# Loads issued inside the layer norms, and three layers of a twelve-layer decoder rearranged

## The chip, the cores and the metric

One Trainium2 chip, one of its cores. The metric is the device time of the whole kernel in microseconds; the median of three runs is 5381.53 us.

## What is computed

A pre-norm decoder of four levels with three layers each, on x of 32 sequences x 64 tokens x 256 features (2048 tokens), in float32:

```python
x = x + L0_attn(norm(x)); x = x + L0_xattn(norm(x), ctx); x = x + L0_ffn(norm(x))
x = x + L1_attn(norm(x)); x = x + L1_xattn(norm(x), ctx); x = x + L1_ffn(norm(x))
x = x + L2_attn(norm(x)); x = x + L2_xattn(norm(x), mask, ctx); x = x + L2_ffn(norm(x))
x = x + L3_attn(norm(x)); x = x + L3_xattn(norm(x), ctx); x = x + L3_ffn(norm(x))
# L0_xattn, a recurrence per channel (k = norm(x), v = ctx), along 64 tokens
no = max(o, u + k); A = exp(o - no); E = exp(u + k - no); y = (A*p + E*v) / (A*q + E)
no2 = max(w + o, k); A2 = exp(w + o - no2); E2 = exp(k - no2)
p, q, o = A2*p + E2*v, A2*q + E2, no2
# L2_ffn: weights are 4-bit codes with one scale per 32 (values 0 .5 1 1.5 2 3 4 6 and a sign)
gelu = tanh(0.79788 * (gate + 0.044715 * gate**3)) * gate * 0.5 + gate * 0.5
out = (gelu * up) @ Wd.T                       # hidden width 2048
# L3_xattn
s = sigmoid(decay) * s + (ctx @ W_in.T + b_in)  # scan over 64 tokens
y = norm(x) + mean(s @ W_out.T + b_out); out = layernorm(y) * gamma + beta
```

## The kernel before

X, XN, XT and CT (the stream, its norm, the norm turned with channels on partitions, and the context turned) stay in SBUF for the whole program. Tokens lie in 16 tiles of 128 or 4 chunks of 512; channels in two halves of 128.
In the layer's Block SyncE issues the loads, and the other engines wait for the sum of them: `attention` (L235, used three times: l0_attn, l1_attn, l2_xattn), `l1_xattn`, `l2_attn`, `l3_attn`, `l3_xattn`, `l3_ffn`. `l3_ffn`, a mixture of experts, issues its small gate weights and then 26 transfers of 384 KB.

`l0_xattn` (L737) runs the recurrence on one channel half after the other, on all 2048 tokens per instruction: a running maximum by one scan, the shifted maximum by a copy (L776), differences, four exponentials on ScalarE, two scans for the sums, denominator, `reciprocal` (L800) on VectorE, numerator, quotient, TensorE transposes (L831), adds into X (L808).

`l2_ffn` (L1702) first turns all codes of gate, up and down weights into float32 on VectorE, nine operations of 2048 elements per nibble and matrix, reloading one pair of buffers between the matrices. Then it loops over 4 chunks and 16 hidden tiles. A unit is: gate and up product (L1815), Square on ScalarE, a scalar and a tensor product on VectorE, Tanh on ScalarE, two more products on VectorE (L1777, L1781), and the down product with the tokens as fixed operand (L1826), one unit late.

`l3_xattn` (L2406) projects the context for 2048 tokens, copies it out, scans it and sums it per sequence, for each channel half; then a loop over 16 tiles broadcasts the means, multiplies by W_out (L2455), adds the bias by a matmul of one row (L2456), adds XN, and normalizes with gain and offset, one tile after the other.

## Time and profile before

| | |
|---|---|
| median of three runs | 5381.53 us (5368.63 to 5385.0) |
| profiled execution, its own time | 5369.39 us |
| its span | 5367.6 us |
| TensorE matmul busy | 4292.7 us, 80% |
| VectorE busy | 3443.4 us, 64% |
| ScalarE busy | 2078.4 us, 39% |
| GpSimd busy | 1218.2 us, 23% |
| mean granted TensorE clock | 0.901 of full speed |

Where the layers begin, by the first statistics of their norm, in us: 36.3, 245.7, 390.9, 505.7, 742.6, 928.3, 1025.6, 1651.8, 2037.0, 2508.5, 4587.6, 4767.9. The shares are averages over layers that have different limits, so a layer is read by its own stretch of the timeline.

### The profile page before, as it was taken

What the parts mean: (1) busy time and instruction counts of PE and PEld (TensorE: products, weight loads), DVE (VectorE), ACT (ScalarE), POOL (GpSimd) and SP (SyncE); (2) the same over time, 40 slices, a digit from 0 to 9 for tenths busy, and PEclk for the clock granted to TensorE, in tenths of its full rate; (3) what the DMA queues carried; (4) which work ended last, traced back from release to release, by engine and by line L of the source; (5) the groups of instructions that cost most, each with busy time, mean ns of one, the idle gap of its engine ahead of it and who ended that gap; (6) DMA issues with size and microseconds to landing.
All of it is one profiled execution on the core that took longest, in us unless ns stands there. A gap on an engine that the chain in (4) does not pass through costs nothing. (4 is left out here: it accounts for less than half of the span.)

```text
span 5367.6 us, 147544 instructions
## 1 busy us (share of the span) xinstructions
PE 4292.7 (80%) x62322; PEld 2855.3 (53%) x62330; DVE 3443.4 (64%) x6320; ACT 2078.4 (39%) x3687; POOL 1218.2 (23%) x1233
## 2 busy tenths in 40 slices
PE   5705777577766881898999999999999999459998
PEld 4603645323324661455576766667676767235554
DVE  4797643678886776544787877778787877331111
ACT  3415442544443551122454544445454444111110
POOL 0100200088893220000222222222222221002222
PEclk9957888788898995998999999999999999559999
DMA  1000000023331001000000000000000000021111
GB/s 45 1 0 33 1 11 0 35 107 121 123 133 37 1 1 47 0 0 18 9 11 11 11 11 13 11 11 11 11 11 11 17 5 3 6 93 52 49 49 47
DMA packets 60767, 157.48 MB, mean 29 GB/s; under 512 B 11890, under 2 KB 19060, under 8 KB 58868
## 3 DMA queue, kind: packets, MB, share of 16 engines
q1 hardware_dynamic: 60180, 148.91, 8.2%
q8 instruction: 459, 7.52, 0.6%
q14 instruction: 128, 1.05, 0.1%
HBM read 146.26 MB, written 2.62 MB: 28 GB/s over the span
## 5 line engine op out<-in xcount | busy, mean ns | idle before, releaser
L2262 POOL TENSOR_TENSOR dn_eb<-dn_ee,dn_cc 128x512 f32<-128x512 f32 x64 | 66.8, 1043 | 1470.0 <-DVE dn_cc L2368 1470.0
L2722 DVE TENSOR_TENSOR moe_hh<-moe_si,moe_pu 128x512 f32<-128x512 f32 x104 | 71.4, 687 | 451.7 <-PE moe_pu L2611 445.4
L1634 POOL TENSOR_TENSOR ssm_ub<-ssm_dtu,ssm_bcn 128x512 f32<-128x512 f32 x256 | 319.5, 1273 | 26.3 <-DVE ssm_ph L1693 24.5
L1986 PE MATMUL dn_bA<-core_XT,dn_w 128*128 128x512 f32 x512 | 268.7, 650 | 45.8 <-issue 40.8
L2298 DVE SCALAR_TENSOR_TENSOR core_XN<-dn_bA,dn_w,core_XN 128x504 f32<-128x504 f32 (+2 forms) x384 | 280.6, 731 | 28.4 <-ACT core_XN L2155 8.8
L2674 POOL TENSOR_TENSOR moe_hw<-moe_hh,moe_cb 128x512 f32<-128x512 f32 x100 | 126.9, 1269 | 681.1 <-DVE moe_hh L2722 393.6
L1595 ACT ACTIVATE ssm_da<-core_XN,ssm_al 128x504 f32<-128x504 f32 x256 | 173.9, 683 | 262.0 <-DVE ssm_ph L1693 142.5
L2655 ACT ACTIVATE moe_si<-moe_pg 128x512 f32<-128x512 f32 x104 | 62.2, 598 | 468.2 <-PE moe_pg L2611 468.2
L2117 PE MATMUL dn_po<-dn_wo,dn_cT 128*128 128x256 f32 x1024 | 239.8, 387 | 1.7 <-ACT dn_cT L2215 1.1
L1532 PE MATMUL ssm_py<-ssm_hc,core_ident 128*128 128x512 f32 x320 | 193.5, 709 | 55.3 <-DVE ssm_hc L1697 30.4
L1693 DVE TENSOR_TENSOR_SCAN ssm_ph<-ssm_da,ssm_ub 128x512 f32<-128x512 f32 x160 | 195.1, 1219 | 53.4 <-ACT ssm_da L1595 22.3
L1815 PE MATMUL nv_pg<-core_XT,nv_wg 128*128 x256 | 122.2, 600 | 116.9 <-PEq L1804 116.9
L2010 PEld LDWEIGHTS dn_pm<-dn_zz,dn_XB 32*32 32x32 f32 x16384 | 165.0, 105 | 93.0 <-issue 91.7
L2245 POOL TENSOR_TENSOR dn_gm<-dn_gg,dn_msk 128x256 f32<-128x256 f32 x128 | 87.5, 703 | 536.6 <-DVEq L2291 534.9
L2010 PEld LDWEIGHTS dn_pm<-dn_XB,dn_mb 32*32 32x32 f32 x16384 | 164.7, 105 | 81.5 <-issue 73.0
L2117 PEld LDWEIGHTS dn_po<-dn_wo,dn_cT 128*128 128x128 f32 x1024 | 190.9, 191 | 28.2 <-ACT dn_cT L2215 1.5
L2268 POOL TENSOR_TENSOR dn_mb<-dn_BD,dn_small 128x256 f32<-128x256 f32 x256 | 190.2, 773 | 50.4 <-DVE dn_BD L2380 50.4
L2611 PE MATMUL moe_pg<-core_XT,moe_w 128*128 128x512 f32 x416 | 198.6, 600 | 0.0
L2010 PE MATMUL dn_pm<-dn_XB,dn_mb 32*32 32x32 f32 x16384 | 193.2, 194 | 6.3 <-DVE dn_XB L2309 3.1
L2611 PE MATMUL moe_pu<-core_XT,moe_w 128*128 128x512 f32 x416 | 196.2, 594 | 0.0
L2010 PE MATMUL dn_pm<-dn_zz,dn_XB 32*32 32x32 f32 x16384 | 193.7, 194 | 1.2 <-ACT dn_zz L2164 1.0
L1532 PE MATMUL ssm_py<-ssm_hp,core_ident 128*128 128x512 f32 x192 | 118.0, 699 | 93.3 <-POOL ssm_hp L1625 93.1
(500 smaller groups left out, 10594.5 us busy)
## 6 DMA issues: line engine op xcount, KB each, us to landing
ssm_bcn<-ssm_bct SPq DMA_DIRECT2D x128, 512.0 KB, 3.6
dn_w<-in_dn_w SPq DMA_DIRECT2D x16, 776.0 KB, 5.3
moe_cb<-moe_rows SPq DMA_DIRECT2D x64, 192.0 KB, 2.8
moe_w<-in_moe_w SPq DMA_DIRECT2D x26, 384.0 KB, 10.5
moe_cb<-moe_rows SPq DMA_DIRECT2D x64, 128.0 KB, 3.0
dn_wo<-in_dn_w SPq DMA_DIRECT2D x16, 256.0 KB, 2.7
moe_cb<-moe_rows SPq DMA_DIRECT2D x64, 64.0 KB, 2.6
core_X<-in_x SPq DMA_DIRECT2D x1, 2048.0 KB, 8.7
```

Source lines behind the costliest of these rows:

```text
L1532: pe.matmul(py[:, turn_ % 2, :], g.ident[:, :], src[:, :], start=n == 0, stop=n == N - 1).then_inc(add_done, 1)
L1595: act.activation(nb(da[:, u % 2, :])[:, :, 1:S], nb(dt[q % 2][:, c, :])[:, :, 1:S], ACT.Exp, scale=al[:, n, c:c + 1]).then_inc(da_ready, 1)
L1634: pool.tensor_tensor(ub[u % NUB][:, :], dtu[q % 2][:, c, :], bcn[i % NB][:, 0, :], ALU.mult).then_inc(ub_ready, 1)
L1693: dve.tensor_tensor_scan(ph[:, m % 2, :], da[:, u % 2, :], ub[u % NUB][:, :], 0.0, ALU.mult, ALU.add).then_inc(scan_done, 1)
L1815: mm = pe.matmul(dst[:, q, :], w[:, kc, cs], g.XT[:, kc, bass.ds(i * CH, CH)], start=kc == 0, stop=kc == DC - 1)
L1986: mm = pe.matmul(bank[:, :], wp[:, kc, gi * P:(gi + 1) * P], g.XT[:, kc, q * CH:(q + 1) * CH], start=kc == 0, stop=kc == DC - 1)
L2010: mm = pe.matmul(bank[r, n * HB:(n + 1) * HB], left(n, r), right(n, r), start=True, stop=True, tile_position=(q * HB, q * HB))
L2117: mm = pe.matmul(po[:, j // 2, (j % 2) * D:(j % 2 + 1) * D], cT[:, 2 * j + h, :], wo[o // NCH % 2][:, h, :], start=h == 0, stop=h == 1)
L2268: pool.tensor_tensor(halves(mb[i % 2][:, l - 1, :]), BD[:, :, :], bcm(small[:, 1 + l, :], NS), ALU.mult).then_inc(mb_ready, 1)
L2298: last = dve.scalar_tensor_tensor(dst[:, :, n:S], src[:, :, 0:S - n], w[i // NCH % 2][:, at:at + 1], dst[:, :, n:S], ALU.mult, ALU.add)
L2611: mm = pe.matmul(dst[:, m % 2, :], w[:, k, at:at + P], g.XT[:, kc, n * CH:(n + 1) * CH], start=kc == 0, stop=kc == DC - 1)
L2674: pool.tensor_tensor(hw[m % 3][:, :], hh[m % 3][:, :], cb[j % NCB][:, :], ALU.mult).then_inc(hw_ready, 1)
```

## The change

- `layer_norm` takes a function `early`, which SyncE runs in the norm's Block. All layers issue their loads by it. Buffers and the semaphores of the loads are made ahead of the norm, in a group of their own; the rest behind it.
- `l0_xattn`: both channel halves in each phase: maxima of both, sums of both, quotients, adds. The shifting copy goes to ScalarE; the reciprocal becomes Ln and Exp(-x) on ScalarE. The load of w and u is issued in the norm.
- `l2_ffn`: the weights are cut into 8 blocks of 256 code columns (all three matrices, both nibbles at once). Blocks 0 and 1 are loaded in the norm. VectorE has six wide operations and four shifts per block, ScalarE two. Tokens go in two halves of two chunks; in the first half the next block is unpacked in four pieces, one in each unit, between the unit's `inner` and `outer`. The down product now has the weights as the fixed operand and 512 tokens as the moving one, two units late; its sums are turned back by transposes (`T` items) at the end of each half.
- `l3_xattn`: four chunks; projection, scan, sum, broadcast, output, statistics and normalization of different chunks overlap; statistics are taken for four tiles at a time; the normalization goes to ScalarE, gain and offset to GpSimd.
- The other layers differ only in where the loads are issued.

```diff
-def layer_norm(nc, g, tag, step=1, turned=True):
+def layer_norm(nc, g, tag, step=1, turned=True, early=None):
...
+            @block.sync
+            def _(sp):
+                if early is not None:
+                    early(sp)
...
+        def early(sp):
+            for dst, name in consts:
+                sp.dma_start(dst[tuple(slice(None) for _ in dst.shape)], w[name]).then_inc(w_loaded, 16)
...
+        layer_norm(nc, g, norm, early=early)
...
+        def early(sp):
+            sp.dma_start(wu[:, :, :], a["wkv_wu"]).then_inc(loaded, 16)
+        layer_norm(nc, g, "0x", early=early)
...
+        om, op, no, a2, e2 = [[s.sb(f"{n}{c}", [P, TOK]) for c in range(DC)] for n in ("om", "op", "no", "a2", "e2")]
+        e1 = [xn[:, c, :] for c in range(DC)]
...
+                def maxima(c):
+                    k = g.XT[:, c, :]
...
                     dve.drain()
+                    dve.tensor_tensor_scan(om[c][:, :], ws[:, :], k, NEG_INIT, ALU.add, ALU.max).then_inc(max_ready, 1)
                     dve.drain()
+                    dve.tensor_tensor(e2[c][:, :], k, om[c][:, :], ALU.subtract)
+                    dve.wait_ge(prev_ready, c + 1)
+                    dve.scalar_tensor_tensor(no[c][:, :], k, u, op[c][:, :], ALU.add, ALU.max)
+                    dve.scalar_tensor_tensor(a2[c][:, :], op[c][:, :], w, om[c][:, :], ALU.add, ALU.subtract).then_inc(decay_ready, 1)
                     dve.drain()
+                    dve.scalar_tensor_tensor(e1[c], k, u, no[c][:, :], ALU.add, ALU.subtract).then_inc(own_ready, 1)
+                    dve.tensor_tensor(no[c][:, :], op[c][:, :], no[c][:, :], ALU.subtract).then_inc(prior_ready, 1)
...
+                def sums(c):
+                    v = g.CT[:, c, :]
+                    dve.wait_ge(exp_ready, c + 1)
...
+                    dve.tensor_tensor(om[c][:, :], no[c][:, :], qb[:, 0:TOK], ALU.mult)
+                    dve.tensor_tensor(om[c][:, :], om[c][:, :], e1[c], ALU.add).then_inc(den_ready, 1)
+                    dve.tensor_tensor(op[c][:, :], no[c][:, :], pb[:, 0:TOK], ALU.mult)
+                    dve.tensor_tensor(tv[:, :], e1[c], v, ALU.mult)
+                    dve.tensor_tensor(op[c][:, :], op[c][:, :], tv[:, :], ALU.add)
+                def quotient(c):
...
+                maxima(0)
+                maxima(1)
+                sums(0)
+                sums(1)
+                quotient(0)
+                quotient(1)
+                added(0)
+                added(1)
...
+                def previous(c):
+                    act.wait_ge(max_ready, c + 1)
+                    act.activation(by_batch(op[c])[:, :, 1:S], by_batch(om[c])[:, :, 0:S - 1], ACT.Copy).then_inc(prev_ready, 1)
...
+                def reciprocals(c):
+                    act.wait_ge(den_ready, c + 1)
+                    act.activation(om[c][:, :], om[c][:, :], ACT.Ln)
+                    act.drain()
+                    act.activation(om[c][:, :], om[c][:, :], ACT.Exp, scale=-1.0).then_inc(rcp_ready, 1)
+                previous(0)
+                exponentials(0)
+                previous(1)
+                exponentials(1)
+                reciprocals(0)
+                reciprocals(1)
...
+    H, BW, NW, NIT = 2048, 256, 3, 3
+    NBLK = H // BW
+    W1 = 2 * NW * BW
...
+        def codes_in(sp, b):
+            for k, n in enumerate("gud"):
+                sp.dma_start(pk[b % 2][:, k, :], a[f"nv_{n}_packed"][:, b * BW:(b + 1) * BW]).then_inc(pk_loaded[b % 2], 16)
+                sp.dma_start(scl[b % 2][:, k, :], a[f"nv_{n}_scales"][:, b * BW:(b + 1) * BW]).then_inc(pk_loaded[b % 2], 16)
+        def early(sp):
+            codes_in(sp, 0)
+            codes_in(sp, 1)
+        layer_norm(nc, g, "2f", step=2, early=early)
...
+                for b in range(2, NBLK):
+                    sp.wait_ge(scaled, b - 1)
+                    codes_in(sp, b)
...
+                for k in range(len(items) + 2):
+                    if k >= 2:
+                        pe.wait_ge(done, k - 1)
+                    if k < len(items) and items[k][0] == "U":
...
+                        gate_up(k, b, (2 * h + i) * CH, n)
+                    if k >= 2 and items[k - 2][0] == "U":
+                        down(k - 2)
+                    if k < len(items) and items[k][0] == "T":
+                        turn(k)
...
+                def parts(b):
...
+                    act.wait_ge(code_ready, b + 1)
+                    if b:
+                        act.wait_ge(w_ready, b)
+                    act.activation(t1[:, :], flat3(mi[:, :, :, :]), ACT.Identity, bias=cst[:, 0:1], scale=2.0).then_inc(part_ready, 1)
+                    act.activation(flat3(sgn[:, :, :, :]), flat3(si[:, :, :, :]), ACT.Identity, bias=cst[:, 1:2], scale=-2.0).then_inc(sign_ready, 1)
+                parts(0)
...
+                def codes(b):
+                    dve.wait_ge(pk_loaded[b % 2], 2 * NW * 16 * (b // 2 + 1))
+                    if b:
+                        dve.wait_ge(w_ready, b)
+                    src = pk[b % 2][:, :, :]
+                    for nib in range(2):
+                        dve.tensor_scalar(mi[:, nib, :, :], src, 4 * nib, 7, ALU.arith_shift_right, ALU.bitwise_and)
+                        dve.tensor_scalar(si[:, nib, :, :], src, 4 * nib + 3, 1, ALU.arith_shift_right, ALU.bitwise_and)
+                    dve.drain().then_inc(code_ready, 1)
+                def sizes(b):
+                    dve.wait_ge(part_ready, b + 1)
+                    dve.scalar_tensor_tensor(t1[:, :], flat3(mi[:, :, :, :]), -2.0, t1[:, :], ALU.add, ALU.max)
+                    dve.drain()
+                    dve.scalar_tensor_tensor(t1[:, :], flat3(mi[:, :, :, :]), 0.5, t1[:, :], ALU.mult, ALU.max)
+                def scales(b):
+                    dve.wait_ge(sign_ready, b + 1)
...
+                    dve.tensor_tensor(both, both, bcm(scl[b % 2][:, :, :].rearrange("p b c -> p (b c)"), 2), ALU.mult).then_inc(scaled, 1)
+                def weights(b):
+                    dve.drain()
+                    dve.tensor_tensor(flat3(w[:, b, :, :, :]), t1[:, :], flat3(sgn[:, :, :, :]), ALU.mult).then_inc(w_ready, 1)
...
+                        inner(k)
+                        if h == 0 and b + 1 < NBLK:
+                            if (i, n) == (0, 0):
+                                codes(b + 1)
+                            if (i, n) == (0, 1):
+                                sizes(b + 1)
+                            if (i, n) == (1, 0):
+                                scales(b + 1)
+                            if (i, n) == (1, 1):
+                                weights(b + 1)
+                        outer(k)
...
+        loads = [(dec, "lk_decay"), (wi, "lk_wi"), (bi, "lk_bi"), (wo, "lk_wo"), (bo, "lk_bo"), (gb, "lk_gb")]
+        nl = 16 * len(loads)
+        def early(sp):
+            for dst, n in loads:
+                sp.dma_start(dst[tuple(slice(None) for _ in dst.shape)], a[n]).then_inc(loaded, 16)
+        layer_norm(nc, g, "3x", turned=False, early=early)
...
+                for n in range(NCH):
+                    for oc in range(DC):
+                        chunk(n, oc)
+                    if n >= 1:
+                        output(n - 1)
+                output(NCH - 1)
...
+                def based_on(i):
+                    pool.tensor_tensor(group(g.X, i), group(g.X, i), bcm(gb[:, 1, :], TPC), ALU.add).then_inc(based, 1)
+                def gain(i):
+                    pool.wait_ge(norm_ready, i + 1)
+                    pool.tensor_tensor(group(g.XN, i), group(g.XN, i), bcm(gb[:, 0, :], TPC), ALU.mult).then_inc(gained, 1)
+                for i in range(NCH):
+                    based_on(i)
+                for i in range(NCH):
+                    gain(i)
...
+                def states(n):
+                    for oc in range(DC):
+                        k = n * DC + oc
+                        dve.wait_ge(xi_ready, k + 1)
+                        dve.tensor_tensor_scan(st[k % 2][:, :], kd[:, :], xi[k % 3][:, :], 0.0, ALU.mult, ALU.add).then_inc(scan_done, 1)
                         dve.drain()
+                        dve.tensor_reduce(ms[:, oc, n * BC:(n + 1) * BC], by_batch(st[k % 2][:, :]), AX.X, ALU.add)
                     dve.drain()
+                    if n >= 2:
+                        dve.wait_ge(y_ready, n - 1)
+                    for oc in range(DC):
+                        last = dve.tensor_scalar(by_batch(mr[n % 2][:, oc, :]), bc(ms[:, oc, n * BC:(n + 1) * BC], S), 1.0 / S, None, ALU.mult)
                     last.then_inc(mr_ready, 1)
+                def stats(i):
+                    dve.wait_ge(y_ready, i + 1)
+                    dve.tensor_tensor(group(g.XN, i), group(g.XN, i), py[:, i % 2, :, :], ALU.add).then_inc(y_done, 1)
                     dve.drain()
+                    for t in range(i * TPC, (i + 1) * TPC):
+                        dve.bn_stats(bs[:, t, :], g.XN[:, t, :])
                     dve.drain()
+                    for t in range(i * TPC, (i + 1) * TPC):
+                        last = dve.bn_aggr(mv[:, t, :], bs[:, t, :])
+                    last.then_inc(stats_ready, 1)
...
+                def added(i):
+                    dve.wait_ge(based, i + 1)
+                    dve.wait_ge(gained, i + 1)
+                    dve.tensor_tensor(group(g.X, i), group(g.X, i), group(g.XN, i), ALU.add)
+                states(0)
+                states(1)
+                stats(0)
+                states(2)
+                means(0)
+                stats(1)
+                states(3)
+                means(1)
+                stats(2)
+                added(0)
+                means(2)
+                stats(3)
+                added(1)
+                means(3)
+                added(2)
+                added(3)
...
+        def early(sp):
+            sp.dma_start(gw[:, :, :], a["moe_gate"]).then_inc(c_loaded, 16)
+            for k in range(G):
+                sp.dma_start(w[:, k, :], a["moe_w"][k, :, :]).then_inc(w_loaded[k], 16)
+        layer_norm(nc, g, "3f", early=early)
```

## Rows read from the trace of the kernel before

**Rows 1.** Timeline, first TensorE instruction of six layers; start, length, idle before.

```profile
58.59 1.87 PE L460 MATMUL a_pm<-a_wo,a_bcol 128*1 128x256 f32 x4 [9.16 <-PEq L296]
...
526.60 3.50 PE L366 MATMUL a_pm<-core_XT,a_wqk 128*128 128x128 f32 x16 [6.95 <-PEq L296]
...
764.55 5.71 PE L1163 MATMUL lin_pr<-core_XT,lin_wq 128*128 128x512 f32 x8 [8.82 <-DMA lin_wo<-in_lin_wo]
...
1049.46 6.61 PE L1501 MATMUL ssm_pp<-core_XT,ssm_win 128*128 128x512 f32 x8 [10.77 <-DMA ssm_vec<-in_ssm_vec]
...
1675.74 3.75 PE L366 MATMUL a_pm<-core_XT,a_wqk 128*128 128x128 f32 x16 [10.82 <-PEq L296]
...
2527.40 13.91 PE L1965 MATMUL dn_po<-dn_wab,core_XT 128*128 128x64 f32 x64 [5.80 <-DMA dn_lt<-in_dn_later]
```

**Rows 2.** Timeline of the recurrence, second channel half.

```profile
327.15 1.76 DVE L768 MEMSET wkv_ws<- 128x2048 f32 x1 [0.38 <-issue]
...
335.07 1.21 DVE L776 COPY wkv_op<-wkv_om 128x2016 f32<-128x2016 f32 x1
...
343.31 1.91 ACT L815 ACTIVATE wkv_a<-wkv_a 128x2048 f32<-128x2048 f32 x1 [54.85 <-ACTq L814]
...
367.89 12.95 DVE L800 RECIPROCAL wkv_om<-wkv_om 128x2048 f32<-128x2048 f32 x1
...
385.50 3.65 PE L831 MATMUL wkv_pt<-core_ident,wkv_yT 128*128 128x128 f32 x16 [59.56 <-PEq L827]
...
389.30 0.69 DVE L808 TENSOR_TENSOR core_X<-core_X,wkv_pt 128x512 f32<-128x512 f32 x1 [0.17 <-DVEq L806]
```

**Rows 3.** The four-bit layer: groups by line, then timeline.

```profile
L1769 DVE TENSOR_SCALAR nv_sq<-nv_sq 128x512 f32<-128x512 f32 x64 | 27.3, 426 | 91.7 <-DVEq L1768 91.5
L1752 DVE SCALAR_TENSOR_TENSOR nv_t<-nv_t 128x2048 f32<-128x2048 f32 x6 | 13.8, 2292 | 0.5
...
2051.89 1.28 ACT L1790 ACT_TABLE_LOAD   x1 [1.47 <-PEq L74]
...
2167.13 3.78 PE L1815 MATMUL nv_pg<-core_XT,nv_wg 128*128 x4 [116.86 <-PEq L1804]
...
2183.14 1.88 PE L1815 MATMUL nv_pg<-core_XT,nv_wg 128*128 x4
...
2188.30 1.88 PE L1815 MATMUL nv_pg<-core_XT,nv_wg 128*128 x4
...
2505.99 1.22 DVE L1786 TENSOR_TENSOR core_X<-core_X,nv_py 128x1024 f32 x1 [2.46 <-DVEq L1783]
```

**Rows 4.** Timeline of the last cross attention: start, cold matmuls, first and last add.

```profile
4599.90 0.34 SPq L2437 DMA_DIRECT2D lk_wi<-in_lk_wi  x1
...
4605.02 8.90 PE L2448 MATMUL lk_pp<-core_CT,lk_wi 128*128 128x512 f32 x16 [22.12 <-DMA lk_dec<-in_lk_decay]
...
4640.47 2.04 PE L2455 MATMUL lk_py<-lk_wo,lk_mr 128*128 128x256 f32 x4 [10.16 <-PEq L2453]
...
4647.49 0.42 DVE L2526 TENSOR_TENSOR core_X<-core_X,lk_z 128x256 f32 x1
...
4766.40 0.42 DVE L2526 TENSOR_TENSOR core_X<-core_X,lk_z 128x256 f32 x1
```

**Rows 5.** Timeline of the last layer's start: SyncE's issues, the first matmuls.

```profile
4782.63 0.33 SPq L2580 DMA_DIRECT2D moe_gw<-in_moe_gate  x1
4783.01 19.01 SPq L2582 DMA_DIRECT2D moe_w<-in_moe_w  x26
...
4784.44 13.86 PE L2598 MATMUL moe_py<-moe_gw,core_XT 128*128 128x32 f32 x64 [3.43 <-DMA moe_gw<-in_moe_gate]
```

**Rows 6.** Tile core_X, last norm: ns minimum, median, maximum; first and last start.

```profile
L154 DVE BATCH_NORM_STATS2 ln3f_st<-core_X x16: 395/410/427, 4767.9 to 4774.9; 128x6 f32<-128x256 f32 x16
```

**Rows 7.** Timeline of l3_attn, VectorE and GpSimd started together.

```profile
3004.88 1.59 POOL L2268 TENSOR_TENSOR dn_mb<-dn_BD,dn_small 128x256 f32<-128x256 f32 x2 [0.79 <-DVE dn_BD L2380]
3004.89 0.99 DVE L2383 TENSOR_TENSOR dn_b<-dn_BD,dn_small 128x256 f32<-128x256 f32 x1
```

567 lines of the change are left out of this document (267 added, 300 removed).

## The prediction

> **What bounds the kernel now.** I read the busy row of the page first, then the listing of one tile (core_X, which every layer reads at its start and writes at its end) to cut the span into layers, then the timeline at each boundary, and for the rebuilt layers the groups by line. TensorE is the busiest engine, but the change touches mostly stretches where it waits: twelve layers stand one behind the other with a barrier of all engines between them, so the time is a sum over layers, and each piece is to be read where it runs. Four kinds of stretch matter. First, behind a normalization the next layer issues its loads and all engines wait for them [rows 1]. Second, the recurrence is a single VectorE chain, twice, with a 12.95 us reciprocal in each [rows 2]. Third, in the four-bit layer TensorE stands idle 116.86 us while VectorE unpacks weights [rows 3]; then it is the bound, one unit of work every 5.16 us. Fourth, in the last cross attention one 128-token tile goes through PE, VectorE, ScalarE and VectorE before the next may start, 16 times [rows 4].
>
> **Early loads, six layers where a wait goes.** PE's idle time before its first instruction was 9.16, 6.95, 8.82, 10.77, 10.82 and 5.80 us [rows 1], 52.3 together. Not all is the load: in the last layer the first issue is at 4782.63, PE starts at 4784.44 and had been idle 3.43, so the barrier takes 1.62 of it [rows 5]. Less 6 x 1.62, 42.6 us go. SyncE issued 26 large transfers in 19.0 us, 0.73 each, so the ten at most of these layers take 7.3, and a normalization lasts 14 (4767.9 [rows 6] to 4782.6): the data are there. I take -42. Bounds: 0 if something else (code, a table) was as late as the data; -47 if TensorE also keeps the high clock it has at the end of a normalization. The two ternary feed-forward layers gain nothing, since VectorE first reduces other data there.
>
> **The loads of the last layer.** Here the early issue costs. SyncE needed 19.0 us to issue 26 weight transfers, from 4783.01 [rows 5]: the issues block. It now does this inside the normalization, whose end is a barrier that includes SyncE. From 4767.9 [rows 6] that is 4767.9 + 0.4 + 19.0 = 4787.3; with the hand-over of 0.9 PE starts at 4788.2, where it started at 4784.44: +3.8 us (bounds: -1.8, the wait for moe_gw alone, if the issues went faster; +6).
>
> **Semaphores.** A scope clears each group of semaphores that it made in a block of its own. Ten layers now make one group more, and 25 or so semaphores are added. Behind the last cross attention a hand-over with one such block takes 4766.82 to 4767.9, 1.1 us [rows 4, 6], so one block costs between 0 and 1.1; I take a third, +3.5 us (bounds 0 and 11).
>
> **The recurrence.** Old: from the second half's start at 327.15 to the last add, 389.30 + 0.69, is 62.8 us, twice 125.7 plus 0.4 between them, 126.1 [rows 2]. Removed from VectorE: two reciprocals (25.9) and two shifting copies at 1.2 (2.4). ScalarE's stand-in for a reciprocal, Ln and Exp, costs 2 x 1.91 and begins when the denominator is ready, with three VectorE operations (6.8 us) and the quotient of the other half still to come: hidden. ScalarE's copy (1.9, as its Exp) runs under the subtraction of 2.3 us: hidden, by 0.2. The transposes and adds behind each half, from 385.50 to 389.99, now overlap for one half: -3.5. The wait for the small load goes, as in the six layers: -1.6, since one transfer lands sooner than ten. Sum -33 (bounds -30, if the hand-overs through ScalarE show, and -35).
>
> **The four-bit layer.** Old: from 2051.89 to 2505.99 + 1.22, 455.3 us [rows 3]. New: the same 64 units of 5.16 us, 330; none of the matmul work changes but the down product, which takes 512 columns with a fixed weight, the same columns. Ahead of it only block 0 is unpacked. A block has 1536 elements per partition and operation. At 2.29 us per 2048 a two-input operation takes 1.72: four of them, 6.9; the four shifts of 768 cost at most 0.43 x 1.5 = 0.6 each, 2.1 together; waiting for ScalarE's part (1536 x 1.91 / 2048 = 1.4) and drains, 2.2. So PE starts 11.2 us into the layer, and its cold start costs 2. Then one block of codes is unpacked per four units. VectorE's own share per unit is 0.43 + 3 x 0.69 = 2.5 (0.69 from the add in [rows 2]), with drains 2.8; four units and a block make 20.0 us, PE's four units 20.6. That is nearly equal, so the order decides. I laid the instructions out one after another: `codes` of the next block lies before the unit's `outer`, ScalarE's two parts (2.9 us) follow and delay the next unit's Square by 2, VectorE idles for that long, then `sizes` (3.5) delays that unit, and the last, `weights`, ends 3 us after PE wanted it. Period 23.5 instead of 20.6, seven times: +20. The half's end (two turns of the sums, each ScalarE's copy 1.0, sixteen transposes 1.9 at the high clock, where they took 3.65 cold [rows 2], and adds 1.4) costs 8.6, the layer's end 7.6. Sum 11.2 + 2 + 330 + 20 + 8.6 + 7.6 = 379: -76. Bounds: if VectorE hid fully, -96; if the 9.0 us of pieces lay fully bare in each block, 7 x (9.0 - 2.9) = 43 more, -33.
>
> **The last cross attention.** Old: from 4599.90 to 4766.40 + 0.42, 166.9 us, of which the 16 rounds are 4766.40 - 4647.49 = 118.9 for fifteen [rows 4]. New, again laid out in order: eight chunks of 4 matmuls. Sixteen took 8.90 us starting cold, five of them at the low clock, so 0.43 each warm: a chunk 1.7. An output step has 24 matmuls of 256 columns: 0.49 each cold (2.04 for four, with a tail), a quarter of 1 us warm, 6 us. PE: 8 x 1.7 + 4 x 6 + 2 = 40. VectorE per group: two scans at 4.42 / 4 = 1.2, two reductions and two broadcasts of 0.7, sum 5.2; statistics 1.2 + 4 x 0.41 + 0.4 = 3.2 (0.41 from [rows 6], the last an estimate); added 1.2: 38 in all. They alternate and end at 43; behind the last output stand the last group's statistics, its Ln and Exp, four ScalarE normalizations (2.1), GpSimd's product (2.4) and an add: 10. So 53. GpSimd now works beside VectorE. A VectorE product of 128x256 that began with two GpSimd instructions took 0.99 us [rows 7], where such a product takes 0.42 [rows 4]; it was held up. Eight GpSimd instructions of some 2.4 us (an estimate: 0.8 for 256 elements in that row, here 1024, less their fixed part) can each hold up one VectorE operation; most fall where VectorE waits anyway, I add 2. Total 55: -112, of which 5 is the load. The Trainium skill, page "SBUF — State Buffer", section "SBUF: two separate sides", speaks against the change here: a GpSimd instruction and a VectorE one that reads two SBUF tensors exclude each other for a whole instruction. By that rule the scans, which read kd and xi from SBUF, wait for up to eight whole GpSimd instructions, and the layer would end at 72 instead of 55; by the row's 0.57 us of delay each it would be 58. Bounds: -117, and, PE at the low clock throughout, 87 us: -80.
>
> **Sum.** -42 + 3.8 + 3.5 - 33 - 76 - 112 = -256, with 2 us for clocks kept high -258, from 5369.4 for the profiled execution (span 5367.6): 5111. The median of the three runs lies 12 us higher, at 5381.5, within a spread of 16; from there it is 5124. I say 5122.
>
> **Rivals.**
> A. TensorE stays at 1.2 GHz in the last cross attention. For it: its output steps are cold today [rows 4]; against: they come after waits, the first of 10.16 us, and would wait 1 us at most. Layer 87 instead of 55: 5154.
> B. VectorE's pieces in the four-bit layer are bare: each block waits through Square, `inner`, a piece, `outer`. For it: the sum is within 3% of PE's. +43: 5165.
> C. The moved loads don't do what they are to: at each layer's start something else is as late. For it: nothing shows what engines would have done without the data; against: the last normalization's first instruction comes 1.1 us behind the add of the layer before, barriers included. +42: 5164.
> D. GpSimd's eight instructions each hold VectorE up for their whole 2.4 us: 19 us instead of the 2 in the sum, +17, 5139. For it: the product that took 0.99 [rows 7]; against: it lost 0.57, not the 0.8 of its neighbour, and VectorE waits for TensorE anyway in part of the layer. This is the case of the Trainium skill's page "SBUF — State Buffer".
> E. Slower than before: the stalls on block hand-overs leave TensorE at the low clock in the four-bit layer. A unit of three groups then takes 10.3 us, and all 64 cost +330: 5122 + 330 = 5452. It decides from 50 units on (258 / 5.16). Against: only 8 of 64 units would have a wait of over 1 us before them.
>
> **How the numbers follow.** Forecast 0.66, A 0.09, B 0.09, C 0.06, D 0.08, E 0.01, no effect or other 0.01. The forecast's own range is 5122 -24 +22: -20 if the blocks hide, -5 clocks; the runs' spread of 16; +11 semaphores and hand-overs. It holds D. For the whole, 5095 to 5158 takes in A and leaves B, C and E out, some 17 in 100. 0.3% of the time is 16 us, which a measurement here can tell from nothing. Faster 0.98, same 0.01, slower 0.01.
>
> **What would show it.** In the profile after: the idle time of PE ahead of the first matmul behind a normalization near 1.6 us in six layers; the last normalization's end at some 19.5 us behind its start; the four-bit layer near 380, its first matmul 11 us in, the block period in its first half 23.5 and the clock at 1.0 there; the last cross attention near 55 with output steps of 6 us; recurrence near 93. Wrong would be made most easily by the order of VectorE's queue in the two pipelined layers, which I laid out by hand with hand-overs of 0.1 to 0.25 us.

## The result, and the profile after

The changed kernel takes 5104.53 us (median of four runs, 5095.46 to 5111.69), the kernel before 5379.23 in the same session: ratio 0.949, 95% interval 0.948 to 0.950, 275 us less. The profiled execution has a span of 5105.5 us against 5367.6 (-262.1) and a mean granted clock of 0.925 in place of 0.901. Forecast were 5122 and 5095 to 5158: the time lies 17 below the first and inside the second.

The span was cut into layers as before, by the first statistics of each norm in the listing of tile core_X (layer and norm together, us; "same kernel again" is after profiled a second time):

| layer | before | after | same kernel again | difference before to after | forecast |
|---|---|---|---|---|---|
| l0_attn | 209.4 | 199.4 | 199.6 | -10.0 | -7.5 |
| l0_xattn (recurrence) | 145.2 | 110.7 | 110.7 | -34.5 | -33 |
| l0_ffn | 114.8 | 115.4 | 115.5 | +0.6 | 0 |
| l1_attn | 236.9 | 229.8 | 226.8 | -7.1 | -5.3 |
| l1_xattn | 185.7 | 182.2 | 177.9 | -3.5 | -7.2 |
| l1_ffn | 97.3 | 96.9 | 96.9 | -0.4 | 0 |
| l2_attn | 626.2 | 616.1 | 616.2 | -10.1 | -9.1 |
| l2_xattn | 385.2 | 377.8 | 377.7 | -7.4 | -9.2 |
| l2_ffn (four-bit) | 471.5 | 385.0 | 384.9 | -86.5 | -76 |
| l3_attn (delta net) | 2079.1 | 2084.9 | 2090.4 | +5.8 | -4.2 |
| l3_xattn | 180.3 | 70.1 | 78.2 | -110.2 | -112 |
| l3_ffn | 599.7 | 601.1 | 600.9 | +1.4 | +3.8 |

The forecast column gives each wait of [rows 1] less 1.62; 3.5 for clearing semaphores and -2 for clocks come to the sum besides.

**Early loads.** Timeline after, the first TensorE instruction of the six layers; the number in brackets is TensorE's idle time before it, which was 5.80 to 10.82 in [rows 1]:

```profile
51.05 1.87 PE L467 MATMUL a_pm<-a_wo,a_bcol 128*1 128x256 f32 x4 [1.80 <-PEq L310]
...
476.55 2.02 PE L373 MATMUL a_pm<-core_XT,a_wqk 128*128 128x128 f32 x16 [1.81 <-PEq L310]
...
706.24 5.37 PE L1198 MATMUL lin_pr<-core_XT,lin_wq 128*128 128x512 f32 x8 [1.66 <-PEq L74]
...
985.41 3.67 PE L1540 MATMUL ssm_pp<-core_XT,ssm_win 128*128 128x512 f32 x8 [1.66 <-PEq L74]
...
1602.41 2.02 PE L373 MATMUL a_pm<-core_XT,a_wqk 128*128 128x128 f32 x16 [1.81 <-PEq L310]
...
2365.42 13.89 PE L2081 MATMUL dn_po<-dn_wab,core_XT 128*128 128x64 f32 x64 [1.66 <-PEq L74]
```

What is left is the barrier. Counted from each norm's start, TensorE begins 7.3, 5.9, 7.1, 8.9, 8.1 and 2.9 us sooner, 40.2 together.

**The last layer** pays, as forecast: SyncE's issues, now in the norm, and the wait in front of the first matmul that they cause (timeline after; [rows 5] has the same before):

```profile
4504.69 17.49 SPq L2729 DMA_DIRECT2D moe_w<-in_moe_w  x26
...
4523.25 13.83 PE L2786 MATMUL moe_py<-moe_gw,core_XT 128*128 128x32 f32 x64 [5.76 <-PEq L74]
```

The norm starts at 4504.4, so TensorE begins 18.9 us behind it; before it was 4784.44 - 4767.9 = 16.5.

**The recurrence.** From 250.78, the instruction at which the 126.1 us of the prediction begin, to the end of the last add at 344.67 it takes 93.9 us (93 forecast). ScalarE's stand-in for the reciprocal waits for VectorE and never the other way round; the adds now are one run of eight:

```profile
250.78 1.76 DVE L774 MEMSET wkv_ws<- 128x2048 f32 x1 [0.40 <-issue]
...
306.07 1.91 ACT L848 ACTIVATE wkv_om<-wkv_om 128x2048 f32<-128x2048 f32 x1 [13.08 <-DVE wkv_om L801]
...
339.81 4.86 DVE L816 TENSOR_TENSOR core_X<-core_X,wkv_pt 128x512 f32<-128x512 f32 x8
```

**The four-bit layer.** Timeline after: the layer's begin, its first matmul, and the waits for the product of the next block ([rows 3] has the layer before):

```profile
1979.66 1.28 ACT L1840 ACT_TABLE_LOAD   x1 [1.46 <-PEq L74]
...
1990.82 3.78 PE L1802 MATMUL nv_pg<-core_XT,nv_w 128*128 128x512 f32 x4 [12.78 <-DVE nv_w L1896]
...
2015.22 1.96 PE L1802 MATMUL nv_pg<-core_XT,nv_w 128*128 128x512 f32 x4 [1.74 <-DVE nv_w L1896]
...
2037.80 1.96 PE L1802 MATMUL nv_pg<-core_XT,nv_w 128*128 128x512 f32 x4 [1.74 <-DVE nv_w L1896]
...
2060.39 1.96 PE L1802 MATMUL nv_pg<-core_XT,nv_w 128*128 128x512 f32 x4 [1.74 <-DVE nv_w L1896]
```

TensorE starts 11.2 us in, as laid out. A later block then takes 22.59 us, 2.0 more than four units, and it always ends with the same wait; the first block, with TensorE cold at its start, takes 24.40.

**The last cross attention.** Timeline after: GpSimd's four additions beside the first scans, two of which are long, and the first output step.

```profile
4446.66 11.29 POOL L2636 TENSOR_TENSOR core_X<-core_X,lk_gb 128x1024 f32<-128x1024 f32 x4 [67.62 <-SPq L2559]
...
4451.19 1.40 DVE L2664 TENSOR_TENSOR_SCAN lk_st<-lk_kd,lk_xi 128x512 f32<-128x512 f32 x1 [1.72 <-ACT lk_xi L2603]
...
4453.28 2.54 DVE L2664 TENSOR_TENSOR_SCAN lk_st<-lk_kd,lk_xi 128x512 f32<-128x512 f32 x1
...
4458.50 1.21 DVE L2664 TENSOR_TENSOR_SCAN lk_st<-lk_kd,lk_xi 128x512 f32<-128x512 f32 x1
```

And windows of that layer (length, busy time with number of instructions of PE, PEld, DVE, ACT, POOL, then the granted clock): the projections start cold, the first output step is at 1.00.

```profile
4446.60:4458.50 11.90, 9.12 (x16) 3.75 (x16) 8.56 (x12) 4.24 (x6) 11.29 (x4) 0.83 0.00 0
4458.50:4469.00 10.50, 10.37 (x33) 5.60 (x34) 7.48 (x16) 0.30 (x1) 0.00 (x0) 1.00 0.01 2
```

### The profile page after: what moved, and what is told of

The parts are those of the page before. It is cut to its first block and busy times, and to the rows that moved or that the text cites. A ratio compares the mean times of both kernels' runs of the same rounds, so it can differ in the third digit from the quotient of the medians.

```text
span 5105.5 us, 146480 instructions
## 1 busy us (share of the span) xinstructions
PE 4270.6 (84%) x62098; PEld 2796.8 (55%) x62106; DVE 3363.6 (66%) x6251; ACT 2120.9 (42%) x3712; POOL 1236.9 (24%) x1241
## 5 line engine op out<-in xcount | busy, mean ns | idle before, releaser
L2414 DVE SCALAR_TENSOR_TENSOR core_XN<-dn_bA,dn_w,core_XN 128x504 f32<-128x504 f32 (+2 forms) x384 | 280.5, 731 | 30.6 <-ACT core_XN L2271 8.8
L2280 ACT ACTIVATE dn_zz<-dn_pm 128x256 f32<-128x256 f32 x320 | 122.6, 383 | 170.0 <-PE dn_pm L2126 158.8
```

The source lines that it names most:

```text
L2414: last = dve.scalar_tensor_tensor(dst[:, :, n:S], src[:, :, 0:S - n], w[i // NCH % 2][:, at:at + 1], dst[:, :, n:S], ALU.mult, ALU.add)
```

## The experiments

Layer times are read as in the table above. Ratios are to the kernel before. All but loads_only, one_clear and best are one execution each, so only their layers are read, not their whole time.

**loads_only.** The kernel after, with the old `l0_xattn`, `l2_ffn` and `l3_xattn`.

> The kernel after, but with the recurrence, the four-bit layer and the last cross attention as they were before, their loads in their own Blocks; the nine other layers issue their loads inside the norm. My theory: each layer is a sum of its own, so this kernel gains what those nine layers gained between the two profiles, 30.7 us (the layers from 0a to 3f without the three: -10.0, +0.6, -7.1, -3.5, -0.4, -10.1, -7.4, +5.8, +1.4), a span near 5337 and a ratio of 0.994. My prediction had -42 for six waits and +3.8 for the last layer, with some +3 for clearing semaphores: -35, 5332. Rival: the delta-net layer's +5.8 hangs on what lies ahead of it (the four-bit layer's end, the clock there); then that layer is back at some 2075 here and the span near 5328. Rival 2: early loads bring nothing by themselves, 5369.

5337.73 us, ratio 0.992 (0.991 to 0.994), span 5334.7, 32.9 less than before. The nine other layers together gained 32.1 (-30.7 between before and after), so the layers together are a sum. Single layers agree less well: l0_attn gained 7.1 here and 10.0 in after, l1_xattn 6.7 and 3.5. The delta-net layer took 2082.5, again longer than before; it does not hang on the four-bit layer ahead of it.

**moe_late.** Only the gate weights are loaded in the last norm:

```diff
         def early(sp):
             sp.dma_start(gw[:, :, :], a["moe_gate"]).then_inc(c_loaded, 16)
-            for k in range(G):
-                sp.dma_start(w[:, k, :], a["moe_w"][k, :, :]).then_inc(w_loaded[k], 16)
...
             def _(sp):
+                for k in range(G):
+                    sp.dma_start(w[:, k, :], a["moe_w"][k, :, :]).then_inc(w_loaded[k], 16)
```

> The kernel after, but the 26 transfers of 384 KB of the last layer are issued in the layer's own Block again; only the gate weights are loaded in the norm. In the profile after, TensorE starts 18.85 us behind the norm's first statistics, with 5.76 us idle before it; before the change it was 16.54. My theory: SyncE's issues hold up the end of the norm's Block; with one issue there the first matmul comes 14.9 us behind the start of the norm, as in the other layers, and the layer takes 597 us in place of 601.1. Rival: the transfers now arrive later than the first groups of weights are wanted, and the gain is given back: layer 600 or more.

The layer took 596.8 us, 4.3 less. Timeline of moe_late:

```profile
4519.61 16.86 SPq L2770 DMA_DIRECT2D moe_w<-in_moe_w  x26
4519.65 13.54 PE L2786 MATMUL moe_py<-moe_gw,core_XT 128*128 128x32 f32 x64 [1.66 <-PEq L74]
```

The 26 issues run beside the gate's matmuls, TensorE starts 14.8 us behind the norm's first statistics in place of 18.9, and none of that is given back later in the layer. So the issue time of a queue counts where its engine must reach a barrier, and here it counted nowhere else.

**one_clear.** A scope clears all its semaphores in one Block, 55 Blocks fewer:

```diff
     def sem(self, *names):
...
-        self.ctx.callback(self.zero, s)
+        self.made += s
+        self.ctx.callback(self.zero)
-    def zero(self, sems):
+    def zero(self):
+        if self.cleared:
+            return
+        self.cleared, sems = True, self.made
```

> The kernel after, but a scope clears all semaphores that it made in one Block when it ends, in place of a Block for each group. 55 Blocks fall away, 33 of them behind the last layer, where from the end of the last add (5084.56) to the issue of the final store (5097.22) 12.66 us pass with 34 such Blocks. My theory: such a Block costs 12.66 / 34 = 0.37 us at most, about what I took (0.35), so -19 to -20 us in all, of which 11 to 12 between the last add and the store; span near 5086, ratio 0.9455. Rival: most of the 12.66 us is the end of the layer's Block and the clearing instructions themselves, which stay; then -5 us or less, span 5100.

5094.14 us, ratio 0.947 (0.946 to 0.949), against 0.949 for after: the intervals overlap, so the profile has to be read. Last adds and final store, first in after, then in one_clear:

```profile
5083.15 1.41 DVE L2901 TENSOR_TENSOR core_X<-core_X,moe_py 128x256 f32<-128x256 f32 x4 [4.44 <-PE moe_py L2814]
5097.22 0.41 SPq L2943 DMA_DIRECT2D out<-core_X  x1
```

```profile
5073.22 1.41 DVE L2906 TENSOR_TENSOR core_X<-core_X,moe_py 128x256 f32<-128x256 f32 x4 [4.43 <-PE moe_py L2819]
5078.11 0.41 SPq L2948 DMA_DIRECT2D out<-core_X  x1
```

12.66 us became 3.48: 9.2 us for 33 Blocks, 0.28 each. Less than the 11 to 12 that I expected, since 3.5 us of the stretch are not these Blocks. The span is 19.1 us below that of after, as I expected, but by luck: the delta-net layer took 10.9 less and the last cross attention 8.6 more, neither of them the Blocks' own time (below). In shifted (below) 20 such Blocks lengthened a hand-over from 2.26 us in best to 8.89, 0.33 each.

**weights_first.** In the four-bit layer the last piece goes ahead of the unit's `inner`:

```diff
+                        if h == 0 and b + 1 < NBLK and (i, n) == (1, 1):
+                            weights(b + 1)
                         inner(k)
```

> The kernel after, but in the four-bit layer the last piece of the next block (weights) lies ahead of the unit's inner in place of behind it. In the profile TensorE waits 1.74 us for that product at each of the blocks 1 to 7, and the period of a block is 22.59 us where four units take 20.6. My theory: the order of VectorE's queue makes the wait; moved ahead of inner (0.43 + 0.69 us and the wait for Square) the product is ready 1.4 us sooner, the wait falls to some 0.4, the period to 21.2 and the layer by 10 us: four-bit layer 375 in place of 385. Rival: VectorE's load is the cause, and the delay only moves into the unit's done, which TensorE waits for two units later: period 22.6 as before. Rival 2: it is better than that, since VectorE also waits for Tanh behind inner: 20.6, -14 us.

The layer took 380.3, 4.7 less; the wait fell from 1.74 to 0.65, but TensorE lost another 0.27 a unit earlier, period 21.87. Half of what I expected. In its timeline VectorE stood idle 2.04 us in each block for a Square that lay behind ScalarE's two parts, and this is what two_orders removes.

**no_beta, beta_twice, beta_late.** GpSimd's additions of the offset in the last cross attention left out, doubled, or placed behind the gains.

> The kernel after, but in the last cross attention GpSimd's four additions of the offset to X are left out (the offset is missing from the output). In the profile after, the first scans take 1.40 and 2.54 us in place of 1.2, two copies of means 1.90 in place of 0.76, and the four GpSimd instructions 2.8 each in place of the 2.35 of the later ones. My theory: the two engines slow each other down in part, some 2 to 3 us of VectorE's time in all, most of it ahead of the first output step; the scans fall to 1.22, the first output starts 2.5 us sooner (it was 11.98 us behind TensorE's first matmul) and the layer from 56 to 53.5. By the rule that a whole GpSimd instruction locks VectorE out, the lost time per scan would have been 2.35, and 4 to 9 us would come back. Rival: TensorE's chunks and not the scans set the start of the first output; then nothing changes.

Layer 67.9, first output at 22.24 us behind the norm's start in place of 24.33; the scans took 1.22 and 1.23. It gave 2.2 of the 2.5 us that I expected for the four additions.

> The kernel after, but GpSimd adds the offset to X twice in the last cross attention (the output has it twice), so four more GpSimd instructions of 2.4 us run beside the second and third groups of scans and the statistics. My theory: each costs VectorE 0.5 us or so, hidden in part by waits for TensorE: +0 to +2 us on the layer. If each locks VectorE out for its whole length, the layer is 5 to 9 us longer. Rival: gain of the first group waits behind the second pass in GpSimd's queue (it ends some 23 us behind the start of the layer, and the first gain was wanted about then), so that only the adds at the end shift, by less than 2 us.

80.2 us, more than any of the expectations, and most of it from a cause that I had not in view: the first output began 2.1 us later and ran at the low clock (1.55, then 2.08 us for four matmuls, in place of 1.13). So this run does not price the additions.

> The kernel after, but GpSimd adds the offset to X of a group behind the gain of that group, and only for the last group ahead of it; nothing of GpSimd lies beside the first scans. My theory: the first output starts 2.5 us sooner, as without the offset, and the four additions lie where VectorE waits for TensorE; the layer ends 1.5 to 2.5 us sooner. Rival: gain, addition, gain of 2.4 us each become late for the adds at the end, and the layer is as long as before or longer by up to 2.4 us.

73.7: longer by 3.6, a miss. The first output did start 2.5 us sooner, but GpSimd met VectorE later. Timeline of beta_late:

```profile
4483.21 2.36 POOL L2636 TENSOR_TENSOR core_X<-core_X,lk_gb 128x1024 f32<-128x1024 f32 x1
...
4483.98 2.67 DVE L2665 TENSOR_TENSOR_SCAN lk_st<-lk_kd,lk_xi 128x512 f32<-128x512 f32 x1 [1.22 <-ACT lk_xi L2603]
...
4492.44 2.35 POOL L2640 TENSOR_TENSOR core_XN<-core_XN,lk_gb 128x1024 f32<-128x1024 f32 x1 [6.87 <-ACT core_XN L2615]
...
4493.25 2.62 DVE L2694 TENSOR_TENSOR core_X<-core_X,core_XN 128x1024 f32<-128x1024 f32 x1
...
4494.75 3.32 POOL L2636 TENSOR_TENSOR core_X<-core_X,lk_gb 128x1024 f32<-128x1024 f32 x1
...
4495.79 2.30 DVE L2689 SCALAR_TENSOR_TENSOR lk_nm<-lk_mv,lk_rs 128x4 f32<-128x4 f32 x1
```

Each waits for the other's end. The scan ends at 4486.65, 1.08 us behind GpSimd's 4485.57, and takes 1.22 alone; the add ends 1.08 behind GpSimd's 4494.79; GpSimd's next takes 3.32 in place of 2.35; and an instruction on 128x4, 0.15 us elsewhere, takes 2.30 behind it. VectorE's add from PSUM (1.22, in after at 4492.56 us) and its statistics (1.41, beside GpSimd in both kernels) lost nothing. The Trainium skill, page "SBUF — State Buffer", section "SBUF: two separate sides", says that whichever of the two starts first holds the pair of ports for its whole instruction; the rows agree.

**dn_late.** The delta-net layer's loads in its own Block again (the old `l3_attn`).

> The kernel after, but the delta-net layer (3a) issues its loads in its own Block, as before. It was the one layer that took 5.8 us longer in the profile after, though TensorE started 2.9 us sooner: the norm took 1.3 more, the stretch from the first matmul to the first add 111.5 in place of 108.9, the 63 periods behind it 1952.1 in place of 1946.6. My theory: nothing of this comes from the moved loads but TensorE's clock after the four-bit layer's end and the loop's branches; then this kernel shows the norm still at 15 us, the loop still within 1946 to 1953, and the layer 2.9 us longer than in after, near 2088. Rival: the shorter wait shifts TensorE's clock in the prologue and the loop for the worse; then the layer is back at 2079 to 2081 here.

2093.5 us, 5.5 more than expected, with the first matmul 20.1 us behind the norm's start (16.0 in after). So the early load gains there too, and the rest, 1957.3 us for the 63 periods, is as long as in kernels that have the early load (1952.1 to 1960.8 in the eight others with as much code ahead of the layer); what lengthens the layer is elsewhere.

**after_again.** The same kernel once more.

> The kernel after once more, nothing changed: what its layers take in a second profile. So far the last cross attention took 70.1 us in after and in moe_late, 78.1 to 80.2 in weights_first, one_clear, dn_late and beta_twice, where TensorE's first output step (16 groups of matmuls, then the next two chunks) runs at the low clock (2.08 us for four matmuls in place of 1.13); in each of the six kernels TensorE had waited 2.0 to 4.8 us for the means ahead of it, and where the wait was 0.22 the clock stayed. The delta-net layer took 2074.0 to 2093.5 in kernels with the same code for it. My theory: whether the clock falls in that wait differs from one execution to the next; then the last cross attention is at 70 or 78 here, and the delta-net layer anywhere from 2080 to 2094. Rival: the same program gives the same clock in each layer; then both repeat within 1 us (70.1 and 2084.9), and the difference comes with each kernel's code.

Last cross attention 78.2, delta net 2090.4, l1_xattn 177.9 in place of 182.2. Timeline of after_again, the first output step and the chunks behind it:

```profile
4456.95 1.61 PE L2580 MATMUL lk_py<-lk_wo,lk_mr 128*128 128x256 f32 x4 [2.04 <-DVE lk_mr L2671]
...
4459.65 2.08 PE L2580 MATMUL lk_py<-lk_wo,lk_mr 128*128 128x256 f32 x4
...
4469.11 6.38 PE L2570 MATMUL lk_pp<-core_CT,lk_wi 128*128 128x512 f32 x8
```

The same instructions take 1.13 and 3.70 us in after. Of the seven profiles with a wait of about 2 us or more ahead of the first output, two kept the clock at 2.4 GHz (waits 2.83 and 2.59, layer 70.1 both) and five fell to 1.2 (waits 1.94 to 2.20, and 4.79 in beta_twice; layer 78.1 to 80.2). Three more kernels, below, fell in a wait of 2.5 to 3.1 us ahead of the fourth step. The length of the wait does not decide it. What TensorE did before it goes with it: in six of the seven profiles the projections begin 12.37 us behind the norm's start and the first output 24.31 to 24.33, and what differs is when the clock rises in between, and so how long the sixteen projection matmuls take. They took 9.12 and 9.35 us in the two that kept the clock, and 9.74, 9.89, 9.89 and 10.01 in the four that lost it; the seventh, beta_twice, had 9.29 and the long wait of 4.79. The chip is not the cause, since moe_late and weights_first ran on one chip with the same code for this layer. First moe_late, then weights_first, each with its first output:

```profile
4447.19 9.35 PE L2570 MATMUL lk_pp<-core_CT,lk_wi 128*128 128x512 f32 x16 [17.70 <-PEq L74]
4459.13 1.13 PE L2580 MATMUL lk_py<-lk_wo,lk_mr 128*128 128x256 f32 x4 [2.59 <-DVE lk_mr L2671]
```

```profile
4443.16 9.89 PE L2570 MATMUL lk_pp<-core_CT,lk_wi 128*128 128x512 f32 x16 [17.70 <-PEq L74]
4455.10 1.63 PE L2580 MATMUL lk_py<-lk_wo,lk_mr 128*128 128x256 f32 x4 [2.05 <-DVE lk_mr L2671]
```

Why the clock rises earlier in one execution than in another stays open. The Trainium skill, page "TensorE: Matmul & The Clock Gate", section "Part 1: The HAM clock gate (the "warmup" mystery)", says that the number of matmuls at the low clock varies from run to run of one kernel; after and after_again show that, with 8 us at stake.

**two_orders.** weights_first, with ScalarE's two parts split over two units; and in the last cross attention the third group projected ahead of the first output step:

```diff
-                    if n >= 1:
-                        output(n - 1)
+                    if n >= 2:
+                        output(n - 2)
```

> The kernel after with two orders changed, in layers that can be read apart. In the four-bit layer, beside weights ahead of inner, ScalarE's second part (the signs, 1.56 us) goes behind the Tanh of the next unit, where weights_first left TensorE waits of 0.65 and 0.27 us a block, period 21.87, with VectorE idle 2.04 us for the Square that stands behind ScalarE's two parts. My theory: that wait falls to 0.5 and the next block is ready in time: period 20.6, layer 371 (385.0 after, 380.3 in weights_first). Rival: VectorE's own load is the limit, period above 21.3. In the last cross attention TensorE projects the third group ahead of the first output step (8 matmuls, 3.4 us), in place of waiting 2 to 2.8 us for the means. My theory: the clock stays at its high level as in no_beta and TensorE works through: layer 67 to 69. Rival: the clock still falls, as it has been high for some 5 us only by then: layer 75 to 78.

Four-bit layer 370.5, as expected (-14.5 against after). TensorE's last waits ahead of the half's end, one for a unit's product in the first block and one for the second block's weights, and then the one at the half's end, in the timeline of two_orders:

```profile
2000.98 1.99 PE L1802 MATMUL nv_pg<-core_XT,nv_w 128*128 128x512 f32 x4 [1.21 <-DVE nv_it L1918]
...
2007.05 1.96 PE L1802 MATMUL nv_pg<-core_XT,nv_w 128*128 128x512 f32 x4 [0.65 <-DVE nv_w L1901]
...
2156.92 0.66 PE L1822 MATMUL nv_pg<-core_ident,nv_yT 128*128 128x128 f32 x4 [1.11 <-ACT nv_yT L1870]
```

Blocks 2 to 7 are ready in time. Last cross attention 75.6, a miss: the first three output steps ran warm, but a wait of 2.50 us now stood ahead of the fourth, which ran cold.

**best.** moe_late, one_clear and two_orders together.

> The kernel after with all that helped: the last layer's 26 transfers in its own Block (measured -4.3 us), one clearing Block for a scope (33 Blocks behind the last layer took 9.2 us, 0.28 each; 22 more elsewhere), and the two orders of two_orders. My theory: -4.3 - 9.2 - 5 for the other clearing Blocks - 14 in the four-bit layer - 5 in the last cross attention (the mean of 0 and 8 that its clock costs, and 1 of wait): -37 against after, 5068 us, ratio 0.942. Rival: the terms hide one another or the delta-net layer's spread of 20 us covers them: 5085 and more.

5069.58 us (5068.35 to 5077.76), ratio 0.944 (0.942 to 0.945), with its interval apart from that of after: 35 us less by the medians, which are of different sessions, and 30 by the ratios, where I expected 37. Last layer 586.7, four-bit layer 370.4; the last cross attention (76.3) had the wait and the cold fourth step of two_orders, so the 5 us that I took for it did not come in this profile.

**shifted.** best, with 20 clearing Blocks ahead of the delta-net layer, and in the last cross attention the last group's `states` ahead of the second group's `stats`.

> The kernel best with two changes in layers that can be read apart. (1) Ahead of the norm of the delta-net layer stand 20 more Blocks in which SyncE clears one semaphore, as many as one_clear took away ahead of that layer, so that the layer's code lies about as far in as in after. In that layer's loop TensorE stands idle at six branches for 36 to 37 us together in before, one_clear, best and loads_only, for 41 to 43 in eight of nine kernels whose code ahead of it is as long as in after, and in those nine (after too) one period of each trip takes 30.6 us in place of 30.3. My theory: the position of the code is the cause; then the idle time is 41 to 43 here and eight periods take 30.6, and the layer, Blocks not counted, takes 2085 to 2092 against 2079.5 in best. Rival: it is the execution, not the position; then idle 36 to 37.5 and no period of 30.6. (2) In the last cross attention best left TensorE a wait of 2.5 us ahead of the fourth output step, behind which that step ran at the low clock (2.08 us for four matmuls), since the last group's states stand behind the second group's statistics; now they stand ahead of them, and ScalarE's inputs of that group ahead of its rstd. My theory: no wait ahead of an output step, all at the high clock (1.13), layer 67 to 69 us in place of 76.3. Rival: the clock falls in a shorter wait somewhere else, layer 73 or more.

(1) Eight periods took 30.6 us again, where best had one and before none; the idle time at the branches was 39.5, between the two kinds, with two branches above 7.4 and none above 6.5 in best. Layer 2083.3, below the 2085 to 2092 that I expected. (2) 76.1: a miss. TensorE now waited 3.11 us for VectorE, and the fourth step again ran cold. Part of the delay is the lock; timeline of shifted:

```profile
4466.25 2.35 POOL L2657 TENSOR_TENSOR core_XN<-core_XN,lk_gb 128x1024 f32<-128x1024 f32 x1 [19.59 <-ACT core_XN L2632]
...
4466.78 2.91 DVE L2681 TENSOR_TENSOR_SCAN lk_st<-lk_kd,lk_xi 128x512 f32<-128x512 f32 x1 [2.71 <-ACT lk_xi L2620]
...
4474.84 2.05 PE L2596 MATMUL lk_py<-lk_wo,lk_mr 128*128 128x256 f32 x4 [3.11 <-DVE core_XN L2693]
```

## Why the prediction was right, and where it was not

**Early loads, -42.** The data were there and the waits fell to 1.66 to 1.81 us, 41.9 less together. At the first matmul 40.2 of them were left, since the transposes of two norms ended later than in before (0.9 us, at the low clock throughout, and 1.2) and those of one 0.8 sooner. The six layers gained only 32.3: the delta-net layer gave back 8.7 behind its first matmul (below) and l1_xattn 3.6, and the other four gained 4.4 more. l1_xattn took 178 to 186 us in kernels with the same code; why is not shown. Rival C falls by the waits themselves, and by loads_only, which is 41.5 us faster by its medians (32.9 by its profile).

**Loads of the last layer, +3.8.** Right in mechanism, too large in size. Against before the first matmul came 2.4 us later (18.9 for 16.5) and the layer took 1.4 more: the 26 issues took 17.49 us where I had 19.0 from [rows 5]. The 4.3 us of moe_late are not this term, since moe_late also keeps the 1.8 us that the early load of the gate weights gains.

**Semaphores, +3.5.** 0.28 and 0.33 us a Block where I took 0.35: an estimated 3 us for ten. Right.

**The recurrence, -33.** -34.5; everything named as hidden was hidden. The stretch itself lost 32.2 us, where the terms inside it sum to 31.8; its start lies 2.9 us nearer to the norm's, where I had 1.6 for the load; 0.9 of this is that the norm's transposes ran at the low clock throughout in before (8.17 us) and only in part in after (7.29).

**The four-bit layer, -76.** It gave 86.5; the mechanism was right, three terms were off. The period was 22.59 in place of 23.5: VectorE did idle 2.05 us for the delayed Square, as laid out, but the last piece held TensorE up by 1.9 us and not by 3; where my layout had the rest is not traced. The first block, cold and 24.4 long though two of its down products come later, took most of this back: 12.0 for six periods and 7.2 for the first (24.4 less 20.6 - 3.4), 19.2 where I had 22. The half's end was mis-sized: I took 8.6 us and forgot that the two `T` items stand among units that keep TensorE busy. The last unit ends at 2337.8; from the last block's start at 2150.74, 36 units of 5.15 bring 2336.1, so it costs 1.6. The layer's end, without the two down products that belong to the units, took 6.1 in place of 7.6. Rival B, the pieces fully bare, falls: it takes some 6 us more a block than four units, and 2.0 were measured. That the order of the queue and not VectorE's load made the period is shown by two_orders.

**The last cross attention, -112.** In the profiled execution -110.2, in the same kernel again -102.1. Where the clock held, its 56.1 us came close to the 55 forecast, with output steps of 6.7 in place of 6. The step that failed is that the output steps "would wait 1 us at most", by which I set rival A aside: the first wait was 2.83. After such a wait TensorE fell to 1.2 GHz in five of seven profiles. It does so for one step and the two chunks behind it, 8 us, and not for the layer, which rival A priced at 32. The expected value is a mean over both, near -104 (an estimate from the seven profiles); that the profiled execution was one of the good ones is luck. For the lock (rival D, 0.08) the single instruction is held for as long as the Trainium skill's page says and not for my 0.57 us from [rows 7]; yet the sum of 2 us was near: the four additions cost 2.2 by no_beta, and of the four products with the gain one held up a VectorE add (1.56 for 1.19). Both are so because a whole-instruction lock costs only where the two engines meet, and in after most of VectorE's operations beside GpSimd come where it waits or read PSUM. beta_late shows the price when they meet more often: 5.8 us more than no_beta, with TensorE's last output only 0.2 later; behind it two adds took 2.61 and 3.35 us in place of 1.2, an instruction on 128x4 elements 2.29, and two of GpSimd's 3.32 in place of 2.35.

**The delta-net layer.** I had forecast -4.2 and it took 5.8 more. By parts: first matmul 2.9 sooner, the stretch to the first add 2.6 longer (TensorE cold for some groups), the 63 periods behind it 5.5 longer, the hand-over 0.6. dn_late clears the moved load. In kernels with as much code ahead of the layer as after, TensorE's idle time at the loop's six branches was 41.1 to 42.9 us in eight of nine, in before, best, one_clear and loads_only 36.1 to 37.4. One branch each of after_again and best:

```profile
2937.51 3.78 PE L2102 MATMUL dn_bA<-core_XT,dn_w 128*128 128x512 f32 x4 [7.44 <-issue]
```

```profile
2927.26 3.40 PE L2112 MATMUL dn_bA<-core_XT,dn_w 128*128 128x512 f32 x4 [6.39 <-issue]
```

The periods of 30.6 us (eight in each of the nine, one at most in before, best and one_clear, but 15 in loads_only) came back in shifted, where of all that concerns this layer only the position of the code differs from best; for the idle time at the branches the run speaks less clearly, and after itself had 37.1. What happens at the branch, the DMA queues of the same profiles show. Their lines of kind "instruction" I take, by that name, as transfers of the program's code. The DMA view of the two waits above, after_again and then best:

```profile
q8 instruction: 2, 0.03, 3.3%
q14 instruction: 3, 0.02, 1.3%
```

```profile
q8 instruction: 1, 0.02, 1.3%
q14 instruction: 2, 0.02, 0.8%
```

Over all 84 branch waits of the 14 profiles, each wait of 7.1 us or more holds two transfers of 16 KB on q8 and each of up to 6.5 holds one, and then ends 1.4 to 1.5 us behind that transfer's end. The extra transfer on q14, within 1.2 us of the wait's start, stands in all 60 waits of the nine kernels and shifted, and in none of before, best and one_clear. The periods of 30.6 us go with q14 too: in the same ten kernels each of the 80 has a transfer on it that starts 23.8 to 24.4 us in, and no period of 30.2 to 30.4 has one there. Shifted has these transfers at the times of after and not of best, though it is one execution, on a chip of its own. So by these records TensorE waits at a branch for code, and the position of the code sets when code is fetched. Why some waits hold a second transfer stays open. Nor does it explain all of after itself: of its 5.5 us the eight periods are 2.4 and the idle time 0.5. That a longer stretch of code ahead of a loop can move it by some us was in no step of mine.

**The sum.** Against the profiled executions it is off by 4 us only (-262 for -258), because the errors cancel, which is luck: the four-bit layer gained 10 more than forecast and l0_attn 2.5, the delta net 10 less. The other 13 us of the 17 lie between profile and median: before's median is 9.8 above its profiled execution (5379.2, 5369.4), after's 2.8 below it (5104.5, 5107.3).

## What to carry to other kernels

A transfer issued ahead of a barrier is paid by its issue time if the issuing engine must reach that barrier; issue early what the next stage waits for at once, and the bulk behind it. When work is laid between the steps of a pipeline, write out the queue of every engine and count the idle of the engine that feeds: here the order alone was worth 14 us in one layer. A wait of 2 us in front of TensorE cost here not 2 us but up to 10, since the clock may fall with it, and one profile doesn't tell; profile the same kernel twice before you explain a layer's time. Where an engine idles at a loop's branch and waits for nothing in the program, look at the instruction lines of the DMA view.

## What was not expected of the hardware

- The same kernel in two profiles: last cross attention 70.1 and 78.2, delta net 2084.9 and 2090.4, l1_xattn 182.2 and 177.9 us, while layers that keep TensorE busy repeat within 0.2.
- A VectorE instruction on 128x4 elements took 2.30 us behind a GpSimd instruction, 0.15 alone; VectorE's copy of the means, one tensor of SBUF to SBUF, was held up too in after (1.90 us for two, 0.76 alone).
- A loop's branch leaves TensorE idle for 5.8 to 7.7 us, with one transfer of code in the shorter waits and two in the longer, and the four matmuls behind it run mostly at the low clock (3.78 us in place of 1.98).
- A Block that only clears semaphores costs 0.28 to 0.33 us.
